# A graph network's attention: one constant product in place of two in each step of the flat softmax pass

## The reference, cut to what matters

```python
logits = (q[dst] * k[src]).sum(-1) * scale + (edge_attr @ ew + eb)
amax = segment_max(logits, dst)
pe = jnp.exp(logits - amax[dst])
ssum = segment_sum(pe, dst)
w = pe / jnp.clip(ssum[dst], 1e-06)
o = segment_sum(w[:, :, None] * v[src], dst)
```

## Time and profile before

| what | value |
|---|---|
| median of 3 runs | 11025.31 us (11010.41 to 11029.87) |
| the profiled execution's own time | 10908.16 us |
| its span, first to last instruction | 10906.4 us |
| mean granted clock of TensorE over the span | 0.728 |
| products of the softmax pass on TensorE | 9749 to 10824 us |
| busy in the stretch from 10600 to 10700 us: TensorE, VectorE, ScalarE, GpSimd | 97.15, 43.67, 67.04, 43.83 us |

### The profile page before, as it was taken

The page is one execution under the profiler, slowest core; times in us unless marked ns, Lnnn a source line. Parts: engine busy times, 40 slices in busy tenths (PEclk is TensorE's granted clock), DMA queues, the critical chain, the costliest instruction groups (busy, mean ns, idle before and its releaser), DMA issues. The chain is left out here.

```text
span 10906.4 us, 254104 instructions
## 1 busy us (share of the span) xinstructions
PE 7146.1 (66%) x50277; PEld 4527.8 (42%) x50278; DVE 5104.3 (47%) x13349; ACT 4538.9 (42%) x7855; POOL 5051.4 (46%) x5161
## 2 busy tenths in 40 slices
PE   3777777777766777777777744444444444449998
PEld 2444444444443444444444432222222222237777
DVE  5444444444454444444444533333334444454445
ACT  2333333333333333333333334444444455546665
POOL 2555555554525555555555334444444444424443
PEclk8788787877887778788888865555555555559999
DMA  4333333333323333333333244444444444436775
GB/s 155 93 94 92 95 93 94 94 89 88 92 64 95 93 95 93 95 94 93 92 89 90 75 127 134 132 131 132 132 132 130 128 126 123 119 107 219 218 218 177
DMA packets 1007773, 1263.10 MB, mean 116 GB/s; under 512 B 307832, under 2 KB 636847, under 8 KB 1006227
## 3 DMA queue, kind: packets, MB, share of 16 engines
q1 hardware_dynamic: 781912, 748.18, 23.3%
q0 software_dynamic: 225792, 514.10, 17.1%
HBM read 1120.15 MB, written 141.53 MB: 116 GB/s over the span
## 5 line engine op out<-in xcount | busy, mean ns | idle before, releaser
L1082 POOL DMA_INDIRECT conv_rows<-src_table,conv_idx x3136 | 3087.1, 984 | 2779.6 <-DMA conv_idx<-in_src_idx 1333.1
L1348 POOL DMA_INDIRECT lg_rows<-kv_table,lg_idx x1568 | 1481.6, 945 | 1970.6 <-issue 1348.0
L922 PE MATMUL ps<-dst_raw,lg_pick 128*128 x5268 | 663.7, 304 | 1765.5 <-ACT lg_pick L907 1522.1
L1185 DVE TENSOR_REDUCE conv_var<-conv_sq 128x32 f32<-128x512 f32 x784 | 536.6, 684 | 2317.5 <-ACT conv_sq L1146 2128.5
L1002 PEld LDWEIGHTS ps<-conv_vals,conv_hot 128*128 128x128 f32 x7024 | 1153.4, 236 | 955.6 <-DVE acc L988 503.1
L1146 ACT ACTIVATE conv_sq<-ps 128x512 f32<-128x512 f32 x784 | 468.1, 597 | 2532.5 <-DMA hidden<-in_x_rows 2036.1
L1002 PE MATMUL ps<-conv_vals,conv_hot 128*128 128x129 f32 x7024 | 1202.0, 325 | 383.3 <-DVE acc L988 313.3
L922 PEld LDWEIGHTS ps<-dst_raw,lg_pick 128*128 x5268 | 522.5, 132 | 2141.3 <-issue 2114.8
L1496 DVE CUSTOM_DVE_ANT_0 acc<-ps,acc 128x512 f32<-128x512 f32 x976 | 649.6, 690 | 1426.4 <-ACT acc L1411 944.9
L1127 PE MATMUL ps<-conv_y,ident 128*128 128x512 f32 x1568 | 1050.7, 758 | 388.5 <-DVE conv_y L1215 369.7
L922 PE MATMUL ps<-dst_raw,conv_pick 128*128 x10536 | 961.7, 240 | 401.8 <-issue 377.3
(11 more groups left out here) (301 smaller groups left out, 10670.6 us busy)
## 6 DMA issues: line engine op xcount, KB each, us to landing
conv_dst<-dst_rows SPq DMA_DIRECT2D x784, 256.0 KB
sm_dst<-dst_rows SPq DMA_DIRECT2D x448, 256.0 KB, 3.7
sm_v<-v_edges SPq DMA_DIRECT2D x448, 256.0 KB, 3.0
acc<-dst_rows SPq DMA_DIRECT2D x392, 256.0 KB
v_edges<-lg_rows SPq DMA_DIRECT2D x392, 256.0 KB
conv_rows<-src_table,conv_idx POOLq DMA_INDIRECT x3136
conv_ea<-ea_parts SPq DMA_DIRECT2D x784, 36.0 KB
lg_rows<-kv_table,lg_idx POOLq DMA_INDIRECT x1568
```

The costliest lines, as they stand in the source:

```text
L922: last = pe.matmul(to[:, j, :], names, part, start=False, stop=False, skip_group_check=True)
L1082: pool.indirect_dma_start(rows[r][:, j, :], None, src_table, bass.IndirectOffsetOnAxis(idx[r][:, j:j + 1], 0)).then_inc(S["rows_in"][r], 16)
L1348: pool.indirect_dma_start(rows[r][:, j, :], None, kv_table, bass.IndirectOffsetOnAxis(idx[r][:, j:j + 1], 0)).then_inc(S["rows_in"][r], 16)
```

## The change

`FILL` goes from 2 to 1. In each step one constant product is issued behind the scatter products, in place of two.

```diff
@@ softmax_pass @@
                 BELOW_AT, LANES, SPARE = (0, 1), 4, 5
-                FILL = 2
+                FILL = 1
                 lanes = bank(LANES)[:, 0:P].unsqueeze(1).to_broadcast([P, TILES, P])
```

## The result

| | kernel before | changed kernel |
|---|---|---|
| median, 4 runs each | 11017.86 us (10982.67 to 11029.87) | 11523.07 us (11510.86 to 11547.22) |
| ratio to before | | 1.0478 [1.0451, 1.0505] |
| profiled execution | 10908.16 us | 11510.86 us |
| mean granted clock over the span | 0.728 | 0.675 |
| first to last scatter of the softmax pass | 1067.3 us | 1583.0 us |

The change makes the kernel 505 us, or 4.8%, slower. The profiled executions are 603 us apart; 516 us of that lie between the first and the last scatter. The pass also begins 88 us later (first L1776 at 9836.70 in place of 9749.17). That difference comes from the passes ahead, which the change does not touch, and it is the reason why the two profiled executions are not subtracted from one another.

A forecast was written before the change was run, and what follows sets the result against it. TensorE was taken as the bound, its clock staying at 1.2 GHz: 442 x 3.527 + 109 x 0.16 = 1576 us against 1067.3, +510 us with the last scatter; 11025.3 + 510 = 11535 us, range 11400 to 11590 us.

The forecast's parts named there:

- The bound: Softmax pass: TensorE is the bound and its step is the pass's step; ScalarE is next with 2.07 us a step.
- The price of one product: Each softmax step: removing one constant product saves 0.426 us at 1.2 GHz, 0.211 us at 2.4 GHz.
- rival 1: Start of softmax pass: clock comes up as before, within 30 us, and holds; 10944 us, 81 us gained; chance 0.12.
- the upper bound of 92: Softmax pass at 2.4 GHz: gain of 92 us if nothing is lost at the loop's turn.
- the half that was taken off at the loop's turn: Loop's turn at 2.4 GHz: half the product's saving discounted in one step of four, 11 us off 92.
- The level: Start of softmax pass: three of four two-product steps failed to raise the clock, so thinner ones stay at 1.2 GHz; 0.80.
- The turn: Loop's turn, once in four steps: 0.16 us extra at 1.2 GHz, 109 times; ends 0 and 0.41 us.
- The 117 us: Whole kernel: median of runs shown, 11025.31 us, lies 117 us above the profiled execution; carried over whole, place unknown.
- Rival 3: Softmax loop: clock, once up, falls now and then; some 200 us loss, 11240 us; chance 0.06 together with late rise.
- the late rise: Softmax pass: clock rises after dozens or hundreds of steps; midway +215 us, 11240 us; chance 0.06 together with falling again.
- Rival 4: Softmax step: product's 0.21 us is hidden in TensorE's wait for its sequencer; no change, 11025 us; chance 0.02.
- What the profile after was to show: Softmax pass: clock 0.50 throughout, scatters 3.53 us apart, eight records 2.16 us, ScalarE under 50%, transfers near 0.48.

## Why the prediction was right

**The bound.** TensorE ends the step at both levels. With the clock down, its step of 3.53 us is the step of the pass, and the waits of ScalarE and GpSimd grew by what TensorE took longer.

**The price of one product.** 0.426 us at the lower level: 3.95 before, 3.53 after, and 3.10 without any. 0.211 us at the upper: half a product less took off 0.10 (2.30 us a step in place of 2.40), and with one in place of two the medians were 82 us (87 without the long execution) and 86 us lower, where 81 were worked out for rival 1. The pass itself was 90 us shorter (977.3 in place of 1067.3 us from first to last scatter), close to the upper bound of 92: the half that was taken off at the loop's turn was not lost.

**The level.** This step decided everything, and it was an argument from three failed steps out of four. It held in all 8 executions of the changed kernel, on two chips. The kernel with the denser start shows the cause, and the one on two rows, like the changed kernel itself, that a TensorE busy without a break is not enough. How much thinner is too thin the argument could not say. By its words one and a half products would have stayed at the lower level too, and that kernel rose within its first step, in its one execution. The start with two products, run again ahead of the thinner loop, took five steps and 19.5 us in place of four and 15.5. So the direction was reasoned, and that one product lies on the far side was in part luck; why one fails and one and a half does not stays open.

**The turn.** 3.70 to 3.73 us against 3.53 to 3.55: 0.17 us, with 0.16 taken and 0 and 0.41 as ends. The step right behind the turn is 0.02 us longer too. 1583.0 us were measured for 442 intervals, against 1576. One count is off, "one product in a step of 26": the step before has 24 products in 29 records, and nothing was worked out from it.

**The 117 us.** They lay between a median and one profiled execution, and carrying them over came out: 11523 us measured, 11535 forecast, 11418 without them. The passes ahead differ by 88 us between the two profiled executions and by nearly 3000 us between chips, so most of them belong there. That could not have been read from the trace; the prediction said so, and the choice was a guess that held.

**The rivals.** Rival 1 needed something that the change lacks, a denser start or a denser turn; given that, its time came, within 10 us. Rival 3, that the thinner warm step does not hold, had been put down to 0.06 together with the late rise. It did not decide here only because the clock never rose, but it is real: one execution in eight of one kernel fell, so did the single one with two products at the start, and the loop without any lost it in some 19 us. My reason against it ("less than a tenth is taken", and no fall in 1050 us) was weak, since the trace of before could not show the margin. Of the nine executions that ran the loop of one product with the clock up, two lost it. Rival 4 is out: at the upper level the product cost its 0.2 us in full, at the turn too.

What the profile after was to show was there: 0.50 to the end, 2.16 us for the eight records, a transfer share of 0.50 (0.48 worked out, and 0.48 in the kernel run again), ScalarE busy 724.02 of 1579 us, 46%. Only the count of constant products was not to be read from the products, but from their loads.

## What to carry to other kernels

Work that keeps TensorE's clock up has a price per step and a benefit that comes all at once: taking half of it away did not give half, it lost the clock and kept the cost. Look at the start of such a pass, not only at its middle: a clock that rose only after four equal steps is a warning, while the steady part shows 1.00 and hides it; how much margin there is only a run tells. Then put the dense work at regular places where the engine idles anyway; the kernel with one product a step and two at the loop's turn took 0.9925 [0.9901, 0.9949] of the time before, and raised the clock by itself.

## What the runs showed of the hardware that was not expected

- Work that did not raise the clock could still hold it. The loop with one product a step never raised it (1583 us at 0.50, TensorE busy throughout), and the same loop kept it at 1.00 for 968 us once it was up.
- A kernel that can hold the upper level but not regain it has two times for one program, 7875 or 8406 us on one chip. Ahead of the one fall of this loop that was traced stood a stumble with 0.28 us of idle TensorE, 0.8 us of delay in all.
- Two constant products at the loop's branch, where TensorE idled for its sequencer, cost nothing: 8.73 against 8.75 us a turn.
- The same program took 11018, 10852, 7962 and 7945 us on different chips. It is the passes ahead that differ: the first L1776 of the pass came at 9749 us in the first trace and at 6807 us on the chip of 7962 us (the kernel with four at the start, whose passes ahead are the same), while the changed kernel's pass took 1583 us on both chips where it ran.
